# Causal attention with a mixture of experts on one core: pieces of TensorE's hand-written order change places, two pieces move on VectorE, and the layer norm is applied by another instruction

## The reference

```python
# attention: 16 heads of 64, causal, on layernorm(x)
sim = jnp.einsum('bhid,bhjd->bhij', q, k) * DH ** (-0.5)
sim = 50.0 * jnp.tanh(sim / 50.0)
sim = jnp.where(causal, sim, jnp.finfo(sim.dtype).min)
attn = jax.nn.softmax(sim, axis=-1)
x = x + out @ Wo.T                       # out: heads of attn @ v, side by side
# feed-forward on t = layernorm(x): one shared layer and 2 of 8 experts
shared = gelu(t @ sw1 + sb1) @ sw2 + sb2
probs = jax.nn.softmax(t @ gate_w + gate_b, axis=-1)
topk_p, topk_i = jax.lax.top_k(probs, 2)
routed = sum over the two chosen experts e of
         topk_p * (gelu(t @ w1[e] + b1[e]) @ w2[e] + b2[e])
x = x + routed + shared
```

## Time and profile before

| | us |
|---|---|
| median of three executions (2067.45 to 2070.11) | 2069.25 |
| the profiled execution | 2068.23 |
| its span, first to last instruction | 2066.5 |
| TensorE busy | 1928.5 (93%) |
| VectorE busy | 1506.6 (73%) |
| ScalarE busy | 1414.9 (68%) |
| GpSimd busy | 1029.5 (50%) |

### The profile page before, as it was taken

One profiled execution on the slowest core, in us unless ns is written; L12 is line 12 of the kernel. 1 busy time (PEld: TensorE's weight loads), 2 busy tenths in 40 slices (PEclk: granted clock), 3 DMA queues, 4 the chain that ended last, 5 costly groups with the idle time before them and its releaser, 6 DMA issues.

```text
span 2066.5 us, 39929 instructions
## 1 busy us (share of the span) xinstructions
PE 1928.5 (93%) x14653; PEld 1519.9 (74%) x14653; DVE 1506.6 (73%) x2786; ACT 1414.9 (68%) x2169; POOL 1029.5 (50%) x1197
## 2 busy tenths in 40 slices
PE   6899999999999999999999999999999974998998
PEld 5676767676767676767676777777777753998998
DVE  5577777777778787878787878787777665665565
ACT  6877777777777777777777777777777742444444
POOL 4444555555555545454545464646464643444444
PEclk9999999999999999999999999999999996999999
DMA  3000000000000000010101010101010125664664
GB/s 134 1 11 11 32 22 32 21 32 21 28 25 26 27 21 32 17 36 15 38 11 42 11 42 11 42 11 42 11 42 1 42 85 167 198 190 133 193 180 140
DMA packets 74653, 112.53 MB, mean 54 GB/s; under 512 B 10713, under 2 KB 53214, under 8 KB 74464
## 3 DMA queue, kind: packets, MB, share of 16 engines
q1 hardware_dynamic: 59456, 67.88, 11.3%
q0 software_dynamic: 15008, 42.10, 5.5%
HBM read 63.09 MB, written 48.65 MB: 54 GB/s over the span
## 4 chain that ended last, share of the span: by engine, by line
PE 83%; ACT 11%; DVE 2%; issue 1%; DMA 1%; POOL 0%; SPq 0%; POOLq 0%; DVEq 0%
PE bank_o L1230 12%; PE ring L1209 7%; PE ring L1136 6%; PE ring L1137 6%; PE ring L1142 6%; PE ring L1214 6%; PE ring L1188 6%; ACT prob L599 3%; PE acc L1253 3%; PE acc L1261 3%; PE acc L1255 3%; PE ring L1195 3%; ACT prob L605 2%; PE bank_d L1244 2%; PE ring L1398 2%; PE ring L1399 2%
## 5 line engine op out<-in xcount | busy, mean ns | idle before, releaser
L515 POOL TENSOR_SCALAR_AFFINE_SELECT prob<-prob 128x256 f32<-128x256 f32 x512 | 229.7, 470 | 544.3 <-ACT prob L605 544.1
L599 ACT ACTIVATE prob<-ring 128x1024 f32<-128x1024 f32 (+1 forms) x384 | 326.4, 875 | 199.9 <-PE ring L1214 196.6
L527 POOL TENSOR_TENSOR key_sum<-prob 128x768 f32<-128x768 f32 x128 | 242.2, 1892 | 212.6 <-PE bank_d L1244 200.2
L605 ACT ACTIVATE prob<-prob 128x1024 f32<-128x1024 f32 (+1 forms) x384 | 342.7, 916 | 5.3
L1230 PE MATMUL bank_o<-prob,v 128*32 128x512 f32 (+3 forms) x4096 | 307.1, 441 | 16.6 <-issue 7.5
L798 DVE TENSOR_TENSOR kT<-ring,kT 64x512 fp32r<-64x512 f32 x256 | 176.2, 688 | 166.9 <-ACT kT L612 164.2
L1209 PE MATMUL ring<-qT,kT 128*128 128x256 f32 (+3 forms) x1024 | 240.0, 336 | 54.4 <-ACT qT L622 19.7
L1209 PEld LDWEIGHTS ring<-qT,kT 128*128 128x128 f32 x1024 | 166.6, 191 | 135.7 <-issue 59.1
L1230 PEld LDWEIGHTS bank_o<-prob,v 128*32 128x32 f32 x4096 | 118.2, 111 | 177.5 <-issue 160.0
L814 DVE RECIPROCAL norm<-bank_d 128x512 f32<-128x512 f32 x64 | 214.9, 3358 | 25.7 <-PE bank_d L1244 24.1
L1214 PE MATMUL ring<-q_lo,kT 128*128 128x256 f32 (+3 forms) x1024 | 229.2, 326 | 1.0 <-DVE q_lo L803 0.9
(11 more groups left out here) (218 smaller groups left out, 4673.5 us busy)
## 6 DMA issues: line engine op xcount, KB each, us to landing
xin<-first SPq DMA_DIRECT2D x71, 257.0 KB, 3.1
xin<-second SPq DMA_DIRECT2D x71, 129.0 KB, 2.5
xin<-base SPq DMA_DIRECT2D x71, 128.0 KB, 2.6
x_next<-in_x SPq DMA_DIRECT2D x16, 512.0 KB, 4.7
x_res<-in_x SPq DMA_DIRECT2D x16, 512.0 KB, 4.0
raw_e<-in_w SPq DMA_DIRECT2D x4, 1024.0 KB, 6.7
first<-pad SPq DMA_DIRECT2D x9, 257.0 KB, 4.4
second<-pad SPq DMA_DIRECT2D x9, 129.0 KB, 6.2
```

The source lines that it names most:

```text
L515: last = nc.gpsimd.affine_select(out=diag, in_=diag, compare_op=ALU.is_ge, fill=0.0, base=0, pattern=[[0, 2], [1, P]], channel_multiplier=-1)
L527: nc.gpsimd.tensor_tensor(sums[:, :, :], t0[:, :, P:N], t13[:, :, 0:N - P], ALU.add).then_inc(sum_steps, 1)
L599: nc.scalar.activation(probs[p % PROBS][u][:, :, :], slot[:, :, 0:UNIT_COLS[u]], ACT.Tanh, scale=SCALE / SOFTCLAMP).then_inc(act_emptied, 1)
L605: nc.scalar.activation(cols, cols, ACT.Exp, scale=SOFTCLAMP).then_inc(exp_done, 1)
```

## The change

On TensorE, in a sequence: values(0) and denominators(0) go from the end of pair 2 to behind scores(3), in the other order; project_out(6) goes from behind scores(2) to ahead of them, project_out(7) from behind the last V tile to ahead of it; project_out(0) goes from behind the projection of pair 4 to ahead of it, project_out(1) from ahead of the projection of pair 5 to behind the gate, project_out(2) from pair 6 to the end of pair 5; hidden and turned logits go ahead of values(3). `denominators` names a wait for the masks, which `values` had named ahead of it. On ScalarE the exp of the gate goes from pair 6 to right behind the gelu and takes the place of the dummy exp. On VectorE the small steps of the second layer norm go from pair 3, behind the weighing of chunk 0, to pair 2, ahead of it. Emptying the logits, weighing chunk 3 and the choice are written in pair 5 instead of pair 6, with nothing between the old place and the new. The layer norms are applied by `scalar_tensor_tensor` with the inverse root broadcast along the row, in place of `tensor_scalar`.

```diff
--- before.py
+++ after.py
@@ -175,7 +175,6 @@
         hT = [x2T[1], x2T[0]]
         row = sb("row", [P, NT, ROW])
         gateT = sb("gateT", [E, N])
-        table_call = sb("table_call", [P, 1])
         b_rows = sb("b_rows", [P, E * D], F32R)
 
         BIAS = E * D // P
@@ -631,7 +630,6 @@
                 for f in range(FC):
                     last = nc.scalar.activation(gelu[:, f, :], slot[:, f, :], ACT.Gelu, bias=b1s[:, f:f + 1])
                 last.then_inc(act_emptied, 1)
-                nc.scalar.activation(table_call[:, :], ones[:, 0:1], ACT.Exp)
 
             def exp_gate(i):
                 act.wait_ge(dve_emptied, EMPTIED[AT["logits", i, 0, 0]][1])
@@ -654,8 +652,6 @@
                 for p in range(PAIRS):
                     clamp(i, p, 2)
                     exponentiate(i, p, 2)
-                    if i >= 1 and p == 6:
-                        exp_gate(i - 1)
                     clamp(i, p, 0)
                     clamp(i, p, 1)
                     exponentiate(i, p, 0)
@@ -683,6 +679,7 @@
                             copy_v(i, t)
                     if i >= 1 and p == 5:
                         hidden_gelu(i - 1)
+                        exp_gate(i - 1)
 
 
             act.wait_ge(ring_full, AT["qk", NSEQ - 1, PAIRS - 1, 0] + 1)
@@ -775,8 +772,9 @@
                 b = ln[which]
                 dve.wait_ge(ln_steps[which], (i + 1) * LN_STEPS)
                 for t in range(NT):
-                    last = nc.vector.tensor_scalar(dst[:, t, :], src[:, t, :], b["mean_var"][:, t, 0:1],
-                                                   b["rstd"][:, t, :], ALU.subtract, ALU.mult)
+                    last = nc.vector.scalar_tensor_tensor(dst[:, t, :], src[:, t, :], b["mean_var"][:, t, 0:1],
+                                                          b["rstd"][:, t, :].to_broadcast([P, D]),
+                                                          ALU.subtract, ALU.mult)
                 last.then_inc(ready, 1)
 
             def empty_turned1(i):
@@ -980,11 +978,9 @@
                         chunk = None
                     if i >= 2 and p == 0:
                         empty_pos(i - 2)
-                    if i >= 1 and p == 6:
-                        empty_logits(i - 1)
                     if i == 0 and p == 3:
                         dve.wait_ge(idle_padded, 16 * 3)
-                    if chunk is not None:
+                    if chunk is not None and p != 6:
                         weigh_values(*chunk)
                     if p == 0 and i >= 2:
                         place_tokens(i - 2)
@@ -992,12 +988,6 @@
                         split_values(*chunk)
                     if p == 2 and i >= 1:
                         split_values(i - 1, PAIRS - 1)
-                    if p == 3 and i >= 1:
-                        layernorm_guess(2, i - 1)
-                        layernorm_newton(2, i - 1)
-                    if p == 6 and i >= 1:
-                        split_hidden(i - 1)
-                        choose(i - 1)
                     if p + 1 < PAIRS:
                         empty_qk(i, p + 1)
                     elif i + 1 < NSEQ:
@@ -1016,6 +1006,8 @@
                         weigh_values(i - 1, PAIRS - 1)
                     if p == 2 and i >= 1:
                         add_attention(i - 1)
+                        layernorm_guess(2, i - 1)
+                        layernorm_newton(2, i - 1)
                     if p == 1 and i + 1 < NSEQ:
                         dve.wait_ge(xnext_loaded, 16 * (i + 2))
                         layernorm_stats(1, x_next)
@@ -1024,6 +1016,13 @@
                         layernorm_apply(1, i + 1, x_next, x_next, xn_ready)
                     if p == 3 and i >= 1:
                         normalise_rows(i - 1)
+                    if p == 5:
+                        if i >= 1:
+                            empty_logits(i - 1)
+                        weigh_values(i, 3)
+                        if i >= 1:
+                            split_hidden(i - 1)
+                            choose(i - 1)
                     if i == 0 and p in LATER_SPLIT:
                         split_lo(LATER_SPLIT[p])
 
@@ -1236,6 +1235,7 @@
                 g = i * PAIRS // 2 + quad
                 if g >= 1:
                     pe.wait_ge(inverted, g)
+                pe.wait_ge(masked, 3 * (2 * g + 1) + 3)
                 for h in range(QUAD):
                     pe.matmul(bank_d[h * QD:(h + 1) * QD, 0:P], ones[:, 0:QD],
                               probs[(2 * quad + h // 2) % PROBS][0][:, h % 2, 0:P], start=True, stop=True)
@@ -1320,14 +1320,19 @@
             pe.wait_ge(xn_hi, 1)
             project_qk(0, 0, (lo_first, 1), (lo_first, 2))
             MIDDLE = {4: turn2, 5: gate, 7: shared_out}
-            LATE = {5: (hidden, turn_logits), 7: (count_earlier,)}
+            LATE = {7: (count_earlier,)}
             for i in range(NSEQ):
                 for p in range(PAIRS):
+                    if p == 2 and i >= 1:
+                        project_out(i - 1, PAIRS - 2)
                     for u in UNIT_ORDER:
                         scores(i, p, u)
-                    if p > 4:
+                    if p == 3:
+                        denominators(i, 0)
+                        values(i, 0)
+                    if p in (4, 7):
                         project_out(i, p - 4)
-                    elif i >= 1 and p < 3:
+                    elif i >= 1 and p < 2:
                         project_out(i - 1, p + 4)
                     if i == 0 and p == 0:
                         project_qk(0, 1, (lo_split, 1), (lo_split, 2))
@@ -1335,10 +1340,15 @@
                         project_qk(i, p + 1)
                     elif i + 1 < NSEQ:
                         project_qk(i + 1, 0)
-                    if p == 4:
-                        project_out(i, 0)
+                    if p == 2 and i >= 1:
+                        project_out(i - 1, PAIRS - 1)
                     if i >= 1 and p in MIDDLE:
                         MIDDLE[p](i - 1)
+                    if p == 5:
+                        project_out(i, 1)
+                        if i >= 1:
+                            hidden(i - 1)
+                            turn_logits(i - 1)
                     if i + 1 < NSEQ and p == 6:
                         turn1(i + 1)
                     if p == 1:
@@ -1348,12 +1358,12 @@
                             pe.wait_ge(v_split, 2)
                     for t in V_UNITS.get(p, ()):
                         project_v(i, t)
-                    if p == 2 and i >= 1:
-                        project_out(i - 1, PAIRS - 1)
-                    if p >= 2:
+                    if p >= 3:
                         values(i, p - 2)
                         if p % 2 == 0:
                             denominators(i, p // 2 - 1)
+                        if p == 5:
+                            project_out(i, 2)
                     elif p == 0 and i >= 1:
                         values(i - 1, PAIRS - 2)
                         denominators(i - 1, PAIRS // 2 - 1)
```

## The result

The changed kernel takes 2084.31 us (median of 5 runs, 2081.12 to 2088.16) where the kernel before took 2070.11 in the same comparison (5 runs, 2067.45 to 2071.89): ratio 1.007, 95% interval 1.0054 to 1.0086. It is slower by 0.7%; I had forecast 2052 and faster. The profiled execution is the median one: 2084.31, span 2082.6.

A forecast was written before the change was run, and what follows sets the result against it. Bound: a TensorE chain, 93% busy, with ScalarE just behind. Pairs 2 to 4 gain 2.0 us, pairs 5 and 6 cost 0.9: 16.5 over 15 sequences plus about 0.5; 2068.23 becomes 2051, median 2052 (range 2038 to 2066).

The forecast's parts named there:

- the walk: Piece-by-piece timing of TensorE's new order in pairs 2 to 6; net gain 1.1 us a sequence.
- I take the low end: VectorE's new layer-norm form beside GpSimd: near 416 ns, not 1,117, and no effect on the sum either way.
- rival (a): New layer-norm form waits for GpSimd; turn2 0.9 late, pair 4 grows about 0.5 us; 2059 us; chance 0.13.
- Rival (b): Moved pieces gain nothing: ScalarE's exps onward run later, hidden 1.1 later than 9.8; 2068 to 2070 us; chance 0.09.
- GpSimd's chain is 1.65 later: Pairs 2 to 4: GpSimd's third key sum waits for denominators(0), leaving 2.5 us of 4.6 slack.
- Cost nothing, as long as that holds.: GpSimd's later sends, masks and sums of pair 3 cost nothing while their 2.5 us of slack lasts.
- rival (c): A send held by 6 us beside VectorE's subtractions makes pair 3's sums late at denominators(1); 2105 us; chance 0.08.
- it does matter: VectorE's normalising now waits for the sends' landing, 1.65 us later; given no price of its own.
- Place 1: Pairs 2 to 4: scores(2) to scores(4) shorten by 1.6 us, pair 4 by 0.4; gain 2.0 a sequence.
- Place 2: Pairs 5 and 6: 27.4 us against 26.65, with a 1.1 wait before hidden; cost taken as 0.9 a sequence.
- The added 0.15 for changes of kind: Pairs 5 and 6: cost raised from 0.75 to 0.9 us for added changes from one kind of matmul to another.
- Sequence 0 has only pair 3's share, about 0.5.: The first sequence gains about 0.5 us, from pair 3 only, against 1.1 in each of 15 others.

The follow-up runs named there:

- k04: Kernel after with the layer norm's application back in the tensor_scalar form in both places: 2058.94 us, ratio 0.9955.
- k09: Kernel after with GpSimd's four second sends directly behind the first sends, in pair 1: 2037.06 us, ratio 0.9868.
- k05: Kernel before with only GpSimd's four second sends moved ahead of its key sum of pair 2: 2175.78 us, ratio 1.0512.
- k10: Kernel after with pairs 5 and 6 ordered as before and the second sends directly behind the first sends: 2032.97 us, ratio 0.9844.
- k02: Kernel before with only the moves of pairs 5 and 6 made, layer norm in the old form: 2073.04 us, ratio 1.0025.
- k03: Kernel after with GpSimd's four second sends ahead of its key sum of pair 2: 2050.16 us, ratio 0.9917.
- k08: Kernel after with a GpSimd memset of 0.31 us ahead of the four second sends: 2078.09 us (one run).
- k12: k03 with values(3) moved ahead of the hidden layer and project_out(2) behind the logits: 2029.53 us, ratio 0.9821.
- k15: k03 with a GpSimd memset of 0.31 us ahead of the second sends: 2040.53 us (one run).
- k11: Kernel after with two of the second sends ahead of the key sum of pair 2 and two behind it: 2036.67 us, ratio 0.9863.

## Why the prediction was wrong

In ratios: forecast 0.992, measured 1.007. Without the long cast 0.9955 (k04), without the held signal as well 0.9868 (k09, which has the new form, but no long cast where hidden waits). So the two unforeseen stops cost 1.15% and 0.87%, 24 and 18 us (23 and 22 when counted up from the traces), and the rest of the walk was 0.5%, 10 us, too pessimistic.

- **"I take the low end. VectorE has waits around both places, so the sum gets nothing from it either way."** This is the step that failed, and it was mis-read, not only mis-sized. The rows took 4.78 us, as in rival (a), 0.7 more than the old form in the same order, and ended 0.42 later, counted from turn2. That alone is 0.4 us. What cost was the cast that this put behind a key sum (2.06 us instead of 0.42, the reciprocal 1.4 later), with hidden placed so that it waits for VectorE. Rival (a) had the stretched form and its 0.9 us at turn2; turn2 showed no wait, and hidden, which I had given 1.1, got 2.2. Rival (b) had the right condition, hidden 1.1 later than 9.8 behind scores(5) (it is 11.0), but from ScalarE. The low end rested on small instructions of the same kind that were never stretched (164 ns); in k05 one of them takes 0.57 us.
- **"GpSimd's chain is 1.65 later"; "Cost nothing, as long as that holds."** The second step that failed. The slack held: denominators(1) never waited for the sums, rival (c) did not come, no send of the sequences took more than 1.23 us. But the sends' new place beside scores(4) cost 1.6 us of TensorE's time in each of the 14 sequences with sends, by a held signal (scores(4) to scores(5) 12.52, 10.95 in k09; the stop itself is printed as 1.32). I had asked what waits for GpSimd, not what else happens while it sends. The landing wait of 2.0 was foreseen only as "it does matter", with no price; by itself it cost nothing: k04 has it too (2.30), and hidden waits 0.87 there.
- **Place 1, 2.0 us.** Right: in k10, where nothing is held, scores(2) to scores(4) take 22.4 (22.1), project_out(6) 1.4 (1.4), and pair 4 gives 0.5 (0.4); 1.83 net.
- **Place 2, 0.9 us.** Right where nothing interferes: hidden 9.7 behind scores(5), scores(6) at 16.84 (16.9), pair 6 10.36 (10.5), 27.20 in all (27.4; before 26.65). The added 0.15 for changes of kind was not there, and pair 1 gave 0.25 back: 0.26 net alone (k02), 0.18 between k10 and k09.
- **"Sequence 0 has only pair 3's share, about 0.5."** Too low: the first bias product, in pair 7 of sequence 1, comes 6.3 us earlier than before (214.66, 220.91), where 1.6 were forecast. 2.0 of it are there when sequence 1 begins (115.00, 117.03). The long wait for the last V copy, with a fallen clock behind it, is in both (3.65 before values(0), 2.82 inside scores(3) of after). The other 4.2 are in sequence 1: in before its scores(4) wait 1.96 for kT and 0.90 for q_lo, and the clock is at its lower level behind that (0.50 in the window 172.2:175.2); in after none of this is there.
- **The signs to look for.** "A wait of more than 2 us before hidden" was named as the mark of a wrong forecast, and it was there.
- Slower had 0.09. The halves of the change could each be walked within 0.2 us; their meeting with a third engine could not be seen in the rows of before, and I gave it too little room.

## What to carry to other kernels

When an order is packed tighter, price the slack of each engine up to the next instruction that TensorE waits for, and then look for casts and two-input instructions of VectorE that start within some tenths of a microsecond of a GpSimd instruction: 0.34 us of lateness became 1.4 us here. Put a burst of indirect sends where TensorE's next signals have nobody waiting for them, and look at it again after every reorder: four sends moved on GpSimd's queue, with nothing else changed, took the same kernel from +0.7% to -1.3% (behind the first sends, k09) or -0.8% (ahead of the key sum, k03), and the latter move in the old order cost 5% (k05). The former was not tried in the old order. A change whose halves measure -0.5% and +0.25% and whose whole measures +0.7% is not refuted; look for what only the whole has.

## What the runs showed of the hardware

Signals of TensorE can be seen late by all that wait for them, until 1.9 to 2.1 us after the start of the last of a group of indirect sends on GpSimd: clamp +1.88 to 1.95 (after), +1.93 to 2.0 (k08), reciprocal +1.95 to 2.07 (k03) and +2.02 to 2.08 (k05). TensorE goes on meanwhile. What decides whether it happens stays open. It isn't the offset between signal and send alone (0.37 held in k03, 0.34 to 0.38 free in k12; 0.07 held in k08, 0.1 free in k15), nor being beside sends at all: in after the first clamp of scores(2) stands between 0.34 ahead of the last first send's start and 0.01 behind it, and is on time in all 14 sequences, and in k11 clamps 0.72 and 1.82 behind the second send are (1079.38, 1080.48). Nor do the DMA packets tell k03 from k12: in both a load of 528 packets runs beside the sends (in after none does), and the sends' own last packet begins 2.06 to 2.3 behind the last send's start. It isn't that packet either: in k08 it begins 2.4 to 3.2 behind in nine sequences, and the clamp still stands at 1.93 to 2.0. Behind the last send of k11 none of the awaited signals is due for 2 us, so it does not test that place. In the kernels with a held signal it is held in all 14 sequences. The Trainium skill (SBUF — State Buffer, Who interferes with whom) says that TensorE and ScalarE never wait for another engine's port; the runs agree as far as TensorE's own work goes, and no run here tells what its signals share with the sends.

The tensor_scalar form with two per-row scalars takes 416 ns for 128x256 alone, the scalar_tensor_tensor with a broadcast 484; beside GpSimd's sums both are stretched, to means of 1,011 and 1,150 in the same order (k04, after).
